# A graph layer and a mixture of experts on one core: experts' weights moved in the load queue, and a tile normalised one step sooner

## The reference

```
z   = layernorm(x)
x1  = x + relu(concat(z @ W_self + b_self, (mask @ z / deg) @ W_nb + b_nb) @ W_comb + b_comb)
n   = layernorm(x1)
logits = n @ Wg + bg               # 8 experts, the best 2 of each row, softmax over the two
y_e = gelu(n @ W1[e] + b1[e]) @ W2[e] + b2[e]
out = x1 + sum over the two chosen e of weight_e * y_e
```

## Time and profile before

| | us |
|---|---|
| median of 3 runs (lowest, highest) | 540.78 (538.82, 542.16) |
| the profiled execution | 538.16 |
| its span in the trace | 536.4 |
| mean granted clock of TensorE | 0.924 of full |

### The profile page before, as it was taken

One profiled execution on the slowest core, in us unless ns is written; L12 is line 12 of the kernel. 1 busy time (PEld: TensorE's weight loads), 2 busy tenths in 40 slices (PEclk: granted clock), 3 DMA queues, 4 the chain that ended last, 5 costly groups with the idle time before them and its releaser, 6 DMA issues.

```text
span 536.4 us, 12757 instructions
## 1 busy us (share of the span) xinstructions
PE 446.0 (83%) x4130; PEld 384.4 (72%) x4130; DVE 395.9 (74%) x1186; ACT 242.4 (45%) x371; POOL 304.1 (57%) x314
## 2 busy tenths in 40 slices
PE   4599889997989979789779799596599999998730
PEld 3489778886868857678668678485489999996620
DVE  2897964746769759769749769788767777789982
ACT  3457642242422423324333333212268889886640
POOL 2579985231334654745644638235777778774570
PEclk9899989998989979989978989799599999999985
DMA  8956999269799799899799798139667555589565
GB/s 255 290 172 181 273 266 265 75 188 269 218 255 275 225 269 270 248 312 260 242 264 240 241 314 227 61 108 270 230 207 232 171 165 184 170 280 397 198 210 157
DMA packets 49168, 122.47 MB, mean 228 GB/s; under 512 B 11081, under 2 KB 20173, under 8 KB 48080
## 3 DMA queue, kind: packets, MB, share of 16 engines
q1 hardware_dynamic: 31632, 68.29, 44.3%
q0 software_dynamic: 16080, 50.49, 31.2%
q10 hardware_dynamic: 1392, 2.88, 1.8%
HBM read 96.52 MB, written 26.93 MB: 230 GB/s over the span
## 4 chain that ended last, share of the span: by engine, by line
DVE 36%; issue 18%; PE 18%; DMA 13%; SPq 7%; ACT 4%; DVEq 3%; POOLq 0%; POOL 0%; ACTq 0%
DMA stage<-in_adj_dram 9%; PE bank L1235 9%; SPq L439 6%; DVE rows L1114 5%; DVE maskT L825 4%; PE bank L1226 3%; PE bank L1227 3%; DMA x_sb<-in_x_dram 2%; DVE w L973 2%; DVE stage L1120 2%; DVEq L392 2%; DVE xh L910 2%; ACT w L722 2%; DVE x_sb L912 2%; DVE mask L818 2%
## 5 line engine op out<-in xcount | busy, mean ns | idle before, releaser
L1226 PE MATMUL bank<-z_flat,maskT 128*128 128x257 f16 x1024 | 240.4, 283 | 0.0
L1227 PE MATMUL bank<-z_lo,maskT 128*128 128x256 f16 x1024 | 240.0, 282 | 0.0
L559 POOL DMA_INDIRECT stage<-in_adj_dram,gidx x64 | 69.5, 1087 | 81.3 <-ACT mask L667 61.4
L1226 PEld LDWEIGHTS bank<-z_flat,maskT 128*128 128x128 fp8e4 x1024 | 103.8, 101 | 15.6
L1227 PEld LDWEIGHTS bank<-z_lo,maskT 128*128 128x128 fp8e4 x1024 | 103.6, 101 | 15.0
L642 POOL DMA_INDIRECT pair_out<-rows,enum x78 | 90.7, 1163 | 36.9 <-issue 20.0
L667 ACT ACTIVATE mask<-stage,m 128x2048 fp8e4<-128x2048 int32 x32 | 64.1, 2003 | 99.2 <-DVE maskT L825 86.3
L570 POOL DMA_INDIRECT dispatched<-rows,slot x64 | 69.0, 1078 | 25.0 <-issue 18.1
L818 DVE TENSOR_SCALAR mask<-stage 128x2048 fp8e4<-128x2048 int32 x32 | 47.5, 1483 | 43.1 <-DMA stage<-in_adj_dram 39.9
L1330 PE MATMUL bank<-stage,w 128*128 128x256 f16 x468 | 59.8, 279 | 5.3 <-DVE stage L1106 5.2
L1350 PE MATMUL bank<-w,stage 128*128 x468 | 57.6, 273 | 2.6 <-DVE stage L1120 2.6
(11 more groups left out here) (179 smaller groups left out, 596.3 us busy)
## 6 DMA issues: line engine op xcount, KB each, us to landing
stage<-in_adj_dram SPq DMA_DIRECT2D x256, 128.0 KB
stage<-dispatched SPq DMA_DIRECT2D x39, 260.0 KB, 3.1
wst<-in_L_ffn_W_dram SPq DMA_DIRECT2D x16, 256.0 KB, 5.4
z_lo<-pair_out SPq DMA_DIRECT2D x4, 1024.0 KB, 6.6
dispatched<-pad SPq DMA_DIRECT2D x15, 260.0 KB, 5.0
out_dram<-x_sb SPq DMA_DIRECT2D x28, 128.0 KB, 5.0
maskT<-pair_out SPq DMA_DIRECT2D x3, 1024.0 KB, 9.1
x_sb<-in_x_dram ACTq DMA_DIRECT2D x6, 256.0 KB, 10.3
```

The source lines that it names most:

```text
L559: gp.indirect_dma_start(out=stage[:, s, b - 2, :], out_offset=None, in_=adj_q[:, :], in_offset=bass.IndirectOffsetOnAxis(ap=gidx[:, 0:1], ...
L1226: mm(acc[u % 2][:, 0:D + 1], a, z_hi[:, i, :], start=(i == 0), stop=False)
L1227: last = mm(acc[u % 2][:, 0:D], a, z_lo[:, i, :], start=False, stop=(i == NT - 1))
```

## The change

It has two parts. In SP's queue `load_expert(k)` for k from 1 to 6 goes from behind `load_adj(4k+3)` to behind `load_adj(4k+5)`, the last one behind all; `load_expert(0)` stays. And a tile is normalised by VectorE in the same step as its x1 and its variance (NORM is 3 and no longer 4). All lags behind it go down by one, on PE, ACT and POOL too, and VectorE's step is written in another order: x1, variance, transpose of the mask, normalise, logits, low part, choice, the experts' pieces, places, and the mask of tile s+2 last. PE sums the ranks in the middle of the neighbours' sum. The early writing of the last but one group's rows stands at step 33 on POOL.

```
-        X1, NORM, LOGIT, SCORE, HOT, SLOT = 3, 4, 5, 6, 9, 11
-        PT, PL, PR = 2, 3, 8
+        X1, NORM, LOGIT, SCORE, HOT, SLOT = 3, 3, 4, 5, 8, 10
+        PT, PL, PR = 1, 2, 7
...
-                if t % B == 3:
-                    load_expert((t - 3) // B)
-
+                if t == B - 1:
+                    load_expert(0)
+                if t >= B + HELD + 1 and t % B == 1:
+                    load_expert((t - HELD - 1) // B)
+
+            load_expert(E - 1)
...
-                    if sent < B * ((s - SLOT + (s == LAST_POWERS - 1)) // B + 1):
+                    if sent < B * ((s - SLOT + (s == LAST_POWERS - 2)) // B + 1):
                         dispatch(sent)
...
             def main_step(t, u, known):
-                if live(known, NORM):
-                    i = t - NORM
-                    dve.wait_ge(s_rs2, i + 1)
...
                 if live(known, X1):
...
                 if HELD <= known < NT:
                     mask_transpose(t, u, known)
-                if HELD <= known < NT - MADE:
-                    masks(t + MADE, u + MADE, known + MADE)
+                if live(known, NORM):
+                    i = t - NORM
+                    dve.wait_ge(s_rs2, i + 1)
+                    if known is None or known - NORM >= 2:
+                        dve.wait_ge(s_hi2, i - 1)
+                    v.tensor_scalar(xh[:, (u - NORM) % 2, :], flat(x_sb, i), mv2[:, (u - NORM) % 4, 0:1], rs[:, at(i)],
+                                    ALU.subtract, ALU.mult).then_inc(s_xh2, 1)
+                if live(known, SCORE):
+                    c = t - SCORE
+                    dve.wait_ge(s_lgp, c + 1)
...
+                if live(known, NORM):
+                    dve.wait_ge(s_hi2, i + 1)
+                    v.tensor_tensor(row16[:, at(i), D:2 * D].rearrange("p o d -> p (o d)"), xh[:, (u - NORM) % 2, :],
...
+                if u % B == HOT % B and live(known, HOT):
+                    choose(div(t, u, known, HOT, B))
                 if u % B == EMAX % B and live(known, EMAX):
...
+                if HELD <= known < NT - MADE:
+                    masks(t + MADE, u + MADE, known + MADE)
...
+                if t < NT:
+                    ranks(t, u, known)
                 if live(known, 0):
                     neighbours(u, 1, known == 0).then_inc(s_mm, 1)
```

More of the change, by code:

```diff
@@ L912, in main_step @@
                     v.scalar_tensor_tensor(flat(x_sb, j), tsum[:, r % 2, :], 0.0, flat(x_sb, j), ALU.max, ALU.add).then_inc(s_x1, 1)
[L913 to L917, removed]
                     dve.wait_ge(s_x1, j + 1)
@@ L927, in main_step @@
                     mask_transpose(t, u, known)
-                if HELD <= known < NT - MADE:
-                    masks(t + MADE, u + MADE, known + MADE)
+                if live(known, NORM):
[8 more added lines that the diff above has]
+                    dve.wait_ge(s_lgp, c + 1)
+                    v.scalar_tensor_tensor(lg[:, (u - SCORE) % B, :], lbank[(u - SCORE) % 2][:, 0:E], scw[:, 3:4], bg_bc[:, :],
+                                           ALU.mult, ALU.add).then_inc(s_lg, 1)
+                if live(known, NORM):
+                    dve.wait_ge(s_hi2, i + 1)
+                    v.tensor_tensor(row16[:, at(i), D:2 * D].rearrange("p o d -> p (o d)"), xh[:, (u - NORM) % 2, :],
+                                    row16[:, at(i), 0:D].rearrange("p o d -> p (o d)"), ALU.subtract).then_inc(s_lo2, 1)
+                if u % B == HOT % B and live(known, HOT):
+                    choose(div(t, u, known, HOT, B))
                 if u % B == EMAX % B and live(known, EMAX):
@@ L935, in main_step @@
                     expert_lo(div(t, u, known, ESPLIT, B))
[L936 to L942, removed]
                 if t == NT + SLOT - 2 * B - 1:
@@ L1279, in main_step @@
                             True, True).then_inc(s_lgp, 1)
-                if t < NT:
-                    ranks(t, u, known)
             pe.wait_ge(s_wf, KT + 2)
```

## The result

The changed kernel took 554.08 us, median of 4 runs (552.92 to 559.09), where the kernel before took 540.7 beside it: ratio 1.027, 95% interval 1.020 to 1.034. The change is slower, in the direction and by the mechanism forecast, and 6 us above the 548 of the forecast, inside the range: 13 us over before where some 7 were forecast. The profiled execution took 552.92, its span 551.1.

The account below looks back on a forecast made before the run. SP's wait for low parts, delaying adj loads, was taken to bound the kernel. Terms +3.2 - 1.1 + 6.4 = +8.5 gave 546.7 on the profiled execution, 549.3 on the median; 548 was taken, range 534 to 556 (forecast's own 542 to 555).

Parts of the forecast that it names:

- What bound before: Middle main steps: SP's wait for the low parts delays adj loads, putting an 8.06 us landing on the chain.
- The floor of the transfers, 35.2: DMA engines' least time for four main steps, 38.3 x 0.92 us; so at most 3.1 us gained a period.
- The loop through POOL, 9.2 us: Steps 10 to 27: pow, normalise, cast, ScalarE's mask, gather, dispatch, next pow; one round takes 9.2 us.
- The signs that I named: Profile after: VectorE waits 15 us or more for pow, DMA share under 0.92, last pow 5 to 6 us after variance.
- The middle, +3.2: Four periods from step 13 to 29: each 39.1 us instead of 38.3, together 3.2 us slower.
- the step with the choice: Once in four steps (s % 4 is 0): VectorE's 10.5 us sets the length, POOL's round with powers being 10.3.
- Rival 3: VectorE's mask meets the gathers, or weights land late: 0.83 us more in each of 16 steps, 562 at most; 7%.
- Steps 4 to 13, -1.1: Early main steps, before and as dispatches start: the transpose of step 13 comes 1.1 us sooner, 178.4 against 179.46.
- The end, +6.4: Transpose of step 29 to normalisation of tile 31: 48.0 us against 41.6, with pow queued behind POOL's dispatches.
- the 6.0: Length in us forecast for step 31, near the end of the main steps.
- From there on nothing differs: After the normalisation of tile 31: no difference up to the choice, and the experts' part shifts as a whole.

Follow-up runs that it names:

- the loads alone: Only the experts' loads moved, against the kernel before, normalisation left as it was: 541.22, 542.07 and 512.41 us in three batches, ratios 0.950, 0.956 and 0.952.
- the second trace of before: The kernel before, unchanged, run and traced again in the third batch: 539.27 us, period 37.7 and end 42.7 us.

## Why the prediction was right, and where its terms were off

**What bound before** was read rightly. The loads' move alone gives 5%, and in the change it takes SP's wait away as said.

**The floor of the transfers, 35.2, was wrong.** I took the share 0.92 times the period for a floor. With the loads alone the same work went in 33.3. There the share makes 1.02 x 33.3 = 34.0 us of transfers in a period, for the same bytes 1.2 less than before; why they took less is open. The gain that the change had to lose was 4.4 to 5.0 us a period, not 3.1. This changed nothing in the forecast, which set the new loop above both.

**The loop through POOL, 9.2 us: right.** It measured 9.2 to 9.4 in the two steps where it decides, with the links as added up. The dispatch ahead of the gather, which opens it, took 4.4 us off the period. I had missed the second loop over TensorE's logits, which is hidden just behind the first. The signs that I named came out too: VectorE waits 29.9 us for pow in all (15 or more forecast), and the DMA share in the middle is 0.88. One was off: the last pow began 3.0 us after its variance (384.79), not 5 to 6.

**The middle, +3.2, was +5.1** (period 39.6 against 39.1), and +7.6 against the second trace of before. The mean steps from 13 to 29 are 10.8, 10.1, 9.4 and 9.2, forecast as 10.5, 10.2, 9.2 and 9.2. The size was off in the step with the choice: I had set POOL there at 10.3, under VectorE's 10.5, and said that a mask which meets its issues is harmless where POOL isn't last. It was last, by one issue of 1.89 in place of 0.98. Rival 3 was a part of the truth, in the step with the choice. The Trainium skill, SBUF — State Buffer, "Who interferes with whom", says that of a VectorE tensor_scalar in a 2-port mode and a GpSimd instruction the one issued first blocks the other for its whole length. This row agrees in kind only: POOL's issue grew by 0.9 us, under the mask's 1.22, and it had begun first. Other rows don't agree: from 100 to 340 us VectorE's mask began within 11 of POOL's issues, and four of these took 0.96 to 0.97 us, one 1.38 and six 1.77 to 1.89. What tells them apart is open.

**Steps 4 to 13, -1.1, were -0.4** (80.9 against 81.3 us), and the first part of the kernel 1.2 longer. The second trace of before has step 4 at 99.05, so most of the 1.2 is no effect of the change. Some 0.4 of the -1.1 was to come ahead of step 4 (97.75 for 98.14), and did not.

**The end, +6.4, was +8.2** (49.8 against the forecast's 48.0; +7.1 against the second trace of before). The steps were 11.7, 9.1, 7.8, 8.7 and 11.35 for 11.7, 9.1 to 9.2, 6.0, 8.6 and 11.2. The one step that failed is the 6.0: I had left POOL's wait for the logits out of its queue. It held four dispatches back by 2.36 us and the pow behind them; with the wait gone, the step took 6.2.

**From there on nothing differs** was right within 0.7 us. The terms add up to +1.2 - 0.4 + 5.1 + 8.2 + 0.7 = 14.8 on the span, measured 14.7, where the forecast's sum was 8.5. Of the 6.2 between them 1.9 come from the middle, 1.8 from the end, and 2.5 from before step 13 and behind the last normalisation, where two traces of one kernel already differ by as much as 1.4 us (179.46 and 180.85 for step 13). So the direction and the loop were foreseen, while the size came out nearly twice as large.

Against the loads alone (512.41, quicker level) the norm part lost 40 us of main steps: 388.39 - 348.05, of which 8 ahead of step 13, 25 in the four periods and 7 at the end. In these steps it gives nothing back: with the loads alone VectorE never waits for pow between steps 13 and 29, so a normalisation one step later held up nothing there.

## What to carry to other kernels

A tile's step taken sooner turns slack between engines into a loop within one step. Before doing so, add up the round over every engine, with each wait in each queue, those for an older tile too: a wait for "four tiles ago" can hang on this step's work. Where a loop goes through a queue of long issues, put the work that nobody waits for where that queue idles anyway. Here that was the dispatch ahead of the gather, 4.4 us in each period. Moving a wait behind other work of the same engine is a cheaper edit to try first: the low parts behind the choice gave 1.2% over the loads alone.

## What the runs showed of the hardware

- A DMA share of 0.92 at 263 GB/s was no ceiling for this mix of SP's and POOL's loads: with the same bytes the middle ran at 300 to 305 GB/s, share 1.02 to 1.04.
- The same program took 537 to 541 us in some batches and 568 in others. At the slower level TensorE showed gaps named issue of up to 1.2 us between matmuls (4.6 us in one step of the loads alone, none in that step at the quicker level), and the experts' part took 19 us or more longer. What sets the level is open. The expectations put it down to the chip, but chip 4 had the slower level in the second batch (568) and the quicker one in the fourth (537). A ratio depended on it: 1.027 and 1.008 for the same change.
- TensorE was busy for 1.1 of the 4.8 us with these gaps, and its granted clock, 1.00 ahead of them, was 0.50 (1.2 GHz) in the 5.7 us behind them.
- An indirect issue of POOL took 1.8 to 1.9 us in place of 1.0 in six of the 11 cases in which VectorE's mask (int32 to fp8, 1.22 us) began within it, in the kernel after from 100 to 340 us. In the loads alone (fourth batch) 13 such issues took 0.99 to 1.38.
